# The last images of a sparse-coding kernel: ScalarE makes the last atoms' coefficient terms, TensorE sums them, and image 14 is added back by DMA

## What is computed

```python
x = x + _L0_conv_ref(_gn(x), ...)            # ternary 3x3 convolution
x = x + _L1_conv_ref(_gn(x), L1_conv_dictionary)
# _L1_conv_ref:
D = dictionary / (norm(dictionary, axis=0) + EPS)
for k in range(1, K_MAX + 1):                # K_MAX = 5
    index = argmax(abs(h * ~mask))           # the next atom of each patch
    ...                                      # progressive Cholesky
    x_stack = solve_triangular(L.T, y)       # coefficients of the k atoms
    h = h_bar - einsum('bk,bkn->bn', x_stack, G[I])
coeffs = zeros((B, N)).at[bidx[:, None], I].set(x_stack)
X_hat = D @ coeffs.T                         # back to patches
```

## Time and profile before

| | |
|---|---|
| median of 3 runs | 542.66 us (541.69 to 544.27) |
| the profiled run | 542.04 us |
| its span in the profile | 540.2 us |
| mean granted TensorE clock | 0.905 |
| busy: PE, DVE, ACT, POOL | 403.2, 457.6, 309.0, 149.2 us |
| HBM read and written | 34.24 MB, 8.65 MB |

### The profile page before, as it was taken

One profiled execution on the slowest core, in us unless ns is written; L12 is line 12 of the kernel. 1 busy time (PEld: TensorE's weight loads), 2 busy tenths in 40 slices (PEclk: granted clock), 3 DMA queues, 4 the chain that ended last, 5 costly groups with the idle time before them and its releaser, 6 DMA issues.

```text
span 540.2 us, 7421 instructions
## 1 busy us (share of the span) xinstructions
PE 403.2 (75%) x1666; PEld 291.6 (54%) x1666; DVE 457.6 (85%) x2323; ACT 309.0 (57%) x682; POOL 149.2 (28%) x162
## 2 busy tenths in 40 slices
PE   0089884999756669999874889998939466788674
PEld 0033772455655656458773755567828355676453
DVE  4574657899799989999999799999998999899990
ACT  2635537876556379778666498676803343465133
POOL 3000035343200064534200655423004644230010
PEclk9999996999779689999996979999979976899598
DMA  5989912799400035999400473413101844134165
GB/s 97 173 101 170 158 39 59 124 161 161 81 0 2 0 88 118 188 178 179 108 1 1 102 171 83 113 40 90 29 1 49 189 113 110 48 78 85 33 116 117
DMA packets 110202, 50.71 MB, mean 94 GB/s; under 512 B 103632, under 2 KB 104144, under 8 KB 110160
## 3 DMA queue, kind: packets, MB, share of 16 engines
q1 hardware_dynamic: 102000, 26.13, 30.9%
q0 software_dynamic: 8160, 24.13, 19.6%
HBM read 34.24 MB, written 8.65 MB: 79 GB/s over the span
## 4 chain that ended last, share of the span: by engine, by line
PE 47%; DVE 35%; ACT 6%; issue 6%; SPq 4%; DMA 1%; DVEq 0%; ACTq 0%
PE h L374 30%; PE conv_ps L374 13%; DVE junk L978 9%; DVE coef L1099 5%; DVE top L908 4%; DVE top_i L921 3%; PE back_ps L374 3%; SPq L241 3%; DVE top_i L923 2%; ACT score L623 2%; ACT diag L632 2%; DVE mask L1005 1%; DVE coef L1095 1%; ACT xb L589 1%; DMA d_sb<-in_L_conv_dictionary 1%
## 5 line engine op out<-in xcount | busy, mean ns | idle before, releaser
L346 POOL DMA_INDIRECT rows<-gram,idx_u x128 | 130.9, 1022 | 334.2 <-DVEq L965 304.7
L374 PE MATMUL h<-rows,diag 128*128 128x256 f32 x640 | 159.7, 408 | 42.3 <-ACT diag L632 41.6
L374 PEld LDWEIGHTS h<-rows,diag 128*128 128x128 f32 x640 | 128.8, 205 | 74.0 <-issue 53.3
L632 ACT ACTIVATE diag<-ident,dx 128x128 f32<-128x128 f32 x320 | 96.8, 388 | 42.1 <-DVEq L1080 39.3
L978 DVE SCALAR_TENSOR_TENSOR junk<-mask,rows 128x256 bf16<-128x256 bf16 x320 | 118.9, 416 | 0.0
L623 ACT ACTIVATE score<-h 128x512 f32<-128x512 f32 x80 | 47.3, 597 | 98.1 <-PE h L374 97.3
L908 DVE MAX8 top<-score 128x8 f32<-128x256 f32 x160 | 65.0, 419 | 22.9 <-ACT score L623 20.9
L374 PE MATMUL back_ps<-coef_t,d_t 128*128 128x256 f32 x224 | 58.3, 419 | 14.5 <-ACT coef_t L638 14.5
L374 PE MATMUL h<-d_sb,z 128*128 128x256 f32 x256 | 66.1, 421 | 3.4 <-DVEq L899 2.5
L374 PEld LDWEIGHTS h<-d_sb,z 128*128 128x128 f32 x256 | 62.8, 329 | 6.7 <-issue 3.2
L374 PE MATMUL conv_ps<-xa,w_taps 128*64 128x512 f32 x128 | 62.7, 613 | 0.1
(11 more groups left out here) (144 smaller groups left out, 491.0 us busy)
## 6 DMA issues: line engine op xcount, KB each, us to landing
xa<-in_x SPq DMA_DIRECT2D x64, 128.0 KB, 4.5
out<-x SPq DMA_DIRECT2D x64, 128.0 KB, 2.9
x<-y POOLq DMA_DIRECT2D x14, 512.0 KB, 4.7
xb<-in_x SPq DMA_DIRECT2D x48, 128.0 KB
rows<-gram,idx_u POOLq DMA_INDIRECT x128, 2.9
xb<-in_x SPq DMA_DIRECT2D x16, 120.0 KB
d_sb<-in_L_conv_dictionary SPq DMA_DIRECT2D x4, 128.0 KB, 4.0
gram<-coef_t SPq DMA_DIRECT2D x1, 256.0 KB, 2.6
```

What stands on the lines that cost most here:

```text
L346: pool.indirect_dma_start(out=rows[s][:, k, t, :], out_offset=None, in_=gram_dram[:, :], in_offset=bass.IndirectOffsetOnAxis(ap=idx_u[s][: ...
L374: return nc.tensor.matmul(dst, lhs, rhs, start=start, stop=stop, skip_group_check=skip)
L632: last = nc.scalar.activation(diag[s][:, t, j, :], ident[:, :], ACT.Copy, scale=dx[s][:, k, t, j:j + 1])
```

## The change

`ACT_TERMS = (2, 2, 1, 1)` gives for each of the last round's four images how many of its last atoms leave DVE's `spread`. ScalarE makes a term for each of them, `terms[m]` = mask times coefficient (`make_terms`; the memory is that of `z`, which is not read any more by then). TensorE's `sum_terms` takes the place of the transposes for these four images: it multiplies terms and coef by the identity with ordinary matmuls that accumulate in PSUM, which transposes and sums at once. DVE signals `x_last_ready` after each x_last. `BY_DMA` becomes 15: image 14 is evicted to y and added to x1 by POOL's DMA; image 15 alone gets its residual in PSUM. Images 14 and 15 swap their places in `h`, and image 15's residual stands where image 14's stood.

```diff
--- before.py
+++ after.py
@@ -52,7 +52,8 @@
     JUNK = 3
     DVE_SQUARES = (1, 3)
     KEPT = 11
-    BY_DMA = IMAGES - 2
+    BY_DMA = IMAGES - 1
+    ACT_TERMS = (2, 2, 1, 1)
 
     ctx = ExitStack()
     with ctx:
@@ -135,6 +136,12 @@
         unread_first = three_images(diag[1][:, :, :, :].rearrange("p t j n -> p (t j n)"))
         iota_i = junk[:, 0:2, :].rearrange("p a n -> p (a n)").bitcast(U32)
 
+        terms = []
+        for m in range(IMG_R):
+            first = 2 * ATOMS * sum(ACT_TERMS[:m])
+            terms.append(z[:, :, :].rearrange("p m n -> p (m n)")[:, first:first + 2 * ATOMS * ACT_TERMS[m]].rearrange(
+                "p (i t n) -> p i t n", t=2, n=ATOMS))
+
         h = [ctx.enter_context(nc.psum_tensor(f"h{s}", [P, TILES, ATOMS], F32)) for s in range(2)]
         conv_ps = ctx.enter_context(nc.psum_tensor("conv_ps", [P, 2, HALF], F32))
         back_ps = [ctx.enter_context(nc.psum_tensor(f"back_ps{b}", [P, 2, 2 * P], F32)) for b in range(2)]
@@ -143,7 +150,7 @@
         def halves(t):
             return [t[:, 0:2, :], t[:, 2:4, :]]
 
-        end_ps = [back_ps, back_ps, halves(h[0]), halves(h[1])]
+        end_ps = [back_ps, back_ps, halves(h[1]), halves(h[0])]
         final_ps = conv_ps[:, 0, :].rearrange("p (k n) -> p k n", k=CHUNKS)
 
 
@@ -194,6 +201,8 @@
         diag_ready = [sem(f"diag_ready{s}") for s in range(2)]
         h_read = [sem(f"h_read{s}") for s in range(2)]
         coef_ready = sem("coef_ready")
+        x_last_ready = [sem(f"x_last_ready{s}") for s in range(2)]
+        terms_ready = sem("terms_ready")
         coef_t_ps = sem("coef_t_ps")
         coef_t_done = sem("coef_t_done")
         recon_ps = sem("recon_ps")
@@ -479,25 +488,37 @@
                 for half in (1, 0):
                     add_atoms(IMG_R * r + m, half, back_ps[half], True)
 
+            def sum_terms(r, m):
+
+                n = IMG_R * r + m
+                pe.wait_ge(terms_ready, m + 1)
+                for i in range(ACT_TERMS[m] + 1):
+                    if i == ACT_TERMS[m]:
+                        pe.wait_ge(coef_ready, n + 1)
+                    for k in range(CHUNKS):
+                        for t in range(2):
+                            part = coef[:, m, t, :] if i == ACT_TERMS[m] else terms[m][:, i, t, :]
+                            last = mm(final_ps[:, k, t * P:(t + 1) * P], part[:, k * P:(k + 1) * P], ident[:, :],
+                                      i == 0 and k == 0 and t == 0, i == ACT_TERMS[m], True)
+                last.then_inc(coef_t_ps, 1)
+
             def last_images():
 
                 r = ROUNDS - 1
                 n = IMG_R * r
                 pe.wait_ge(h_read[0], STEPS * ROUNDS)
                 for half in (1, 0):
-                    residual(n + 2, half, end_ps[2][half])
+                    residual(n + 3, half, end_ps[3][half])
                 for m in range(2):
-                    coef_transposes(r, m, final_ps)
+                    sum_terms(r, m)
                     for q, half in enumerate((1, 0)):
                         pe.wait_ge(y_done, 2 * (n + m) + q + 1)
                         add_atoms(n + m, half, end_ps[m][half], True)
                 pe.wait_ge(h_read[1], STEPS * ROUNDS)
-                for half in (1, 0):
-                    residual(n + 3, half, end_ps[3][half])
                 for m in range(2, IMG_R):
-                    coef_transposes(r, m, final_ps)
+                    sum_terms(r, m)
                     for half in (1, 0):
-                        add_atoms(n + m, half, end_ps[m][half], False)
+                        add_atoms(n + m, half, end_ps[m][half], m == 2)
 
             for m in range(IMG_R):
                 conv(0, m)
@@ -762,7 +783,28 @@
             for r in range(1, ROUNDS - 1):
                 body(r, True, True)
             body(ROUNDS - 1, False, True)
-            for m in range(IMG_R):
+
+            def make_terms(r, m):
+
+                s = m // 2
+                act.wait_ge(x_last_ready[s], ROUNDS)
+                for i in range(ACT_TERMS[m]):
+                    j = STEPS - ACT_TERMS[m] + i
+                    for t in range(2):
+                        tile = 2 * (m % 2) + t
+                        last = nc.scalar.activation(terms[m][:, i, t, :], mask[s][:, j - 1, tile, :], ACT.Copy,
+                                                    scale=x_last[s][:, tile, j:j + 1])
+                last.then_inc(terms_ready, 1)
+
+            make_terms(ROUNDS - 1, 0)
+            make_terms(ROUNDS - 1, 1)
+            copy_coef(ROUNDS - 1, 0, final_ps)
+            out_back(ROUNDS - 1, 0, end_ps[0])
+            copy_coef(ROUNDS - 1, 1, final_ps)
+            make_terms(ROUNDS - 1, 2)
+            make_terms(ROUNDS - 1, 3)
+            out_back(ROUNDS - 1, 1, end_ps[1])
+            for m in range(2, IMG_R):
                 copy_coef(ROUNDS - 1, m, final_ps)
                 out_back(ROUNDS - 1, m, end_ps[m])
 
@@ -1079,14 +1121,17 @@
                 if k < STEPS - 1:
                     dve.sem_inc(dx_ready[s], 1)
                 else:
-                    step(v.tensor_reduce(x_last[s][:, :, :], dx[s][:, :, :, :].rearrange("p k t j -> p t j k"), AX.X, ALU.add))
+                    c = step(v.tensor_reduce(x_last[s][:, :, :], dx[s][:, :, :, :].rearrange("p k t j -> p t j k"), AX.X, ALU.add))
+                    yield
+                    after(c)
+                    dve.sem_inc(x_last_ready[s], 1)
 
             def spread(r, m):
 
                 s = m // 2
                 if r > 0:
                     dve.wait_ge(coef_t_ps, IMG_R * (r - 1) + m + 1)
-                for j in range(STEPS):
+                for j in range(STEPS - ACT_TERMS[m] if r == ROUNDS - 1 else STEPS):
                     added = []
                     for t in range(2):
                         tile = 2 * (m % 2) + t
```

## The result

| | median, us | runs | ratio to before (95%) |
|---|---|---|---|
| before | 542.38 (541.04 to 544.27) | 6 | |
| the change | 546.74 (546.39 to 548.91) | 6 | 1.009 [1.0063, 1.0117] |

A forecast was written before the change was run, and what follows sets the result against it. The prediction took DVE's chain of waits over the last 41 us, then image 15's stores, as the bound. From the profiled 542.04 - 0.75 + 0.1 = 541.4, with the median 0.6 above, it forecast 542.0 us, range 539.9 to 544.4.

The forecast's parts named there:

- I take 0.05 ... and three earlier rounds lose some 0.1 us together: DVE after x_last: the signal's wait, 0.05 us between bounds 0 and 0.23; some 0.1 us for three earlier rounds.
- I take 4.95: Tail: image 14's add by POOL's DMA lands 4.95 us after issue, between rows of 4.49 and 5.86.
- the place where the end would hang: Tail: image 15's stores queue on SyncE behind image 14's, which wait for its add; the end moves 0.75 us earlier.
- ScalarE's terms: ScalarE, last round: twelve mask-times-coefficient terms at 0.40 us each, bounds 0.3 and 0.61.
- the small matmul: TensorE, last round: each ordinary matmul by the identity takes 0.25 us, 0.45 at the low clock.
- DVE's eight updates: DVE ahead of images 14 and 15's last step: eight updates dropped at 0.398 us each, 3.18 us on the chain.
- the clock's return: TensorE in the tail: gapless work from 501.0 brings the clock high at about 506.2, after 5.2 us.
- that image 15's stores wait for SyncE: Tail: SyncE needs 2.6 us for image 14's stores, so image 15's leave at 533.9 though ready at 532.65.
- rival 1: TensorE in the tail: clock low until 512, or dearer small matmuls, set the end and slow it to 543.9; chance 0.27.
- Rival 2: Image 14's add lands in under 3.7 us, so image 15's stores don't wait: 540.8 us; chance 0.15.
- Rival 3: DVE's 3.2 us do not arrive because something else holds images 14 and 15's last step: 544.7 us; chance 0.05.
- The "slower" case: Whole kernel slower than 545.4 us, from small matmuls above 0.35 us or rival 3 with a late add; chance 0.08.

The follow-up runs named there:

- e2: The change, with the signal on x_last given in the last round only: 543.63 us, ratio 1.0011.
- e14: The kernel before, with e9's constant matmuls and the signal after each x_last, which nobody waits for: 537.20 us, ratio 0.9904.
- e9: The kernel before, with unread constant matmuls in TensorE's gaps at each round's boundary and in the last round: 536.59 us, ratio 0.9862.
- e1: The kernel before, with the signal after each x_last and nothing that waits for it: 549.22 us, ratio 1.0118.
- e15: The kernel before, with the unread signal on x_last issued two DVE operations later in every round: 543.05 us, ratio 1.0015.
- e13: The change, with the signal on x_last issued two DVE operations later in every round: 542.75 us, ratio 1.0007.
- e12: e2, with image 15's stores issued by ScalarE instead of by SyncE behind image 14's: 543.58 us, ratio 1.0015.
- e11: e2, with DVE adding images 14 and 15 from PSUM, image 15 summed in a second PSUM bank, and e9's constant matmuls: 529.50 us, ratio 0.9747.

## Why the prediction was wrong

**The step that failed first is the signal: "I take 0.05 ... and three earlier rounds lose some 0.1 us together".** The bounds, 0 to 0.23, were right, and the value is the upper one at all six places ahead of the last round. (Six times 0.05 would have been 0.3 and not 0.1.) The text ahead of the prediction says that the change touches the last 40 us; six of its eight signals lie ahead of them. The reason given, "in most places another operation is in the pipe", was wrong: the wait is for the operation just issued, and one that went in before it is no cover. At the bound, six signals are 1.4 us; measured, they cost 3.6. The Trainium skill ("VectorE: DVE Perf Modes", "The DRAIN you can't avoid") reports eight copies taking 13.88 us with a semaphore after each as with one after the last, and says that it costs nothing extra; here it costs 0.23 us each time, as DVE's operations otherwise start before the one ahead has ended (0.23 us behind a reduce that lasts 0.32).

**A term was missing beside it:** what a late DVE sets off in the earlier rounds. I followed the clock in the tail alone. TensorE waits on DVE in the gaps of each round, and the six signals cost 3.6 us by the medians (change against e2), 2.5 times their own delay. e14 against e9 points to the clock for the rest: with TensorE kept busy, eight signals cost 1.2 to 2.3 us instead of 6.4. e1's mean clock, 0.894 against e15's 0.905, goes the same way. The change's hardly does: 0.903 against the 0.905 and 0.913 of e2 and e13, which have nearly its tail, and 0.898 to 0.901 before. At the same mean clock it is still slower: its four runs at 0.902 to 0.905 took 546.4 to 546.8 us, e2's three there 542.8 to 545.3, and those of the kernel before 541.0 to 543.2. So the clock's part is argued and not measured. Why a DVE that is 0.24 us late makes the clock lower on the mean, rather than lower in some runs and higher in others, is not settled; nor is why e1's eight cost 6.4 us and the change's six 3.6.

**The second step that failed: "I take 4.95" for the landing of image 14's add.** It took 6.09, above both rows. The interpolation went by how far image 13's stores were ahead, 1.8 us; they were 1.33, since image 13's add itself took 5.15 us and not the 4.5 of "image 12's stores are over". With 5.15 and 6.09 and the store row, the forecast of the tail in terms of the first x_last closes: image 14's eviction 0.6 us later than forecast (of which 0.5 is DVE's: x_last ready at 17.7 instead of 17.2, from the signal's wait of 0.23 and the pause of 0.3 behind it), the add 1.1, the last stores' landing 0.2, together 2.0 = 1.24 + 0.75. e2 and e13, without the loss ahead of the tail, stand at +0.8 and +0.5 us: without those signals the change is worth nothing that can be measured, for that reason.

**Right:** the place where the end would hang (image 14's add, then its stores, then image 15's); ScalarE's terms, 0.41 us for 0.40; the small matmul, 0.22 for 0.25, and 0.45 at the low clock; DVE's eight updates; the clock's return, 6.5 us after the first x_last for 7.4 (it rose 4.4 us after the first small matmul at 506.28; before, 5.1 us after the first atoms at 507.00); image 13's eviction, 21.3 us after that x_last for 20.9; image 14's and 15's evictions at 27.8 and 34.0 for 27.2 and 33.8. The transposes turned matmuls were not the danger. **Half right:** that image 15's stores wait for SyncE; they wait there, but e12 shows that the end comes no earlier when they don't.

**The rivals:** rival 1's place did not occur (the clock was up before image 12's atoms), though its mechanism, a lower clock on TensorE, likely had its part elsewhere. Rival 2's quick add is excluded by 4.52 us at the least, and with it the estimate of 3.2 us from the Trainium skill ("DMA: Bandwidth & Descriptors"). Rival 3 did not happen. The "slower" case had been given 0.08, from small matmuls or a late DVE; the mechanism that came was in none of the three.

## What to carry to other kernels

Price a signal at every place that runs it, not where it is read: guard it by the round that needs it, or issue it two operations later (worth 3.6 to 3.9 us here, for two lines). The second only helps where other operations do come between: see in the trace that they do, since at half 1's places here none did. Before giving a part of the tail to an adding DMA, count its whole hop and the stores it meets; an engine that is idle by then can add from PSUM in 1.1 us. Where TensorE's gaps cost it the clock, matmuls of constants in them are worth trying first: alone they gave more (6.3 us) than the whole change could have.

## What the runs showed of the hardware that was not expected

- DVE starts its next operation 0.23 us into a reduce of 0.32; waiting for that reduce first makes it 0.46, 0.14 us after the reduce's end.
- Runs of one kernel differ by their clock: of the change's six, the two slowest (548.59 and 548.91 us) had a mean granted clock of 0.892 and 0.895, the other four (546.39 to 546.77) 0.902 to 0.905.
- An adding DMA of 512 KB lands in 4.5 us alone, 5.2 beside the end of four stores and 6.1 behind four fresh ones; a store of 128 KB takes 2.8 us at the end of the queue and 4.5 to 5.0 with eight on their way.
- DVE adds 128x512 from PSUM to SBUF in 1.05 to 1.10 us, the same as ScalarE's eviction (1.07), so it can take that work over at no loss while it is idle. One of e11, in order of time:

```profile
521.18 1.05 DVE L1332 TENSOR_TENSOR x<-h,x 128x512 f32<-128x512 f32 x1 [0.64 <-PE h L386]
```
